# Rotary products of a row issued one head earlier, in an attention and expert kernel on one Trainium2 core

## What is computed

```python
ct_q  = _lin(x, w_down_q, b_down_q)                        # x is the normalised row
q_ct  = _lin(ct_q, w_up_q, b_up_q)
rope_q = _rope(_lin(ct_q, wq_r, bq_r), cos, sin)
q = (q_ct + rope_q).reshape(bs, sl, nh, hd)                # 16 heads of 16
ct_kv = _lin(x, w_down_kv, b_down_kv)
k_ct  = _lin(ct_kv, w_up_k, b_up_k)
rope_k = _rope(_lin(ct_kv, wk_r, bk_r), cos, sin)
k = (k_ct + rope_k).reshape(bs, sl, nh, hd)
v = _lin(ct_kv, w_up_v, b_up_v).reshape(bs, sl, nh, hd)
scores = jnp.einsum('bqhd,bkhd->bhqk', q, k) / np.sqrt(hd)
probs = jax.nn.softmax(scores, axis=-1)
a = jnp.einsum('bhqk,bkhd->bqhd', probs, v)
```

## Time and profile before

| | us |
|---|---|
| median of 3 runs | 497.55 (495.1, 497.55, 499.42) |
| profiled execution, its own time | 496.64 |
| its span in the profile | 494.8 |
| mean granted TensorE clock | 0.97 |
| PE busy | 436.1 (88% of the span) |
| DVE busy | 252.4 (51%) |
| ACT busy | 185.6 (38%) |
| POOL busy | 134.7 (27%) |

### The profile page before, as it was taken

How to read it: one execution, slowest core, us unless ns; L and a number is a source line. 1 busy time by engine, 2 the same in 40 slices (tenths; PEclk the granted TensorE clock), 3 DMA queues, 4 the chain that set the end, 5 groups by cost and what they waited for, 6 DMA issues and landing times.

```text
span 494.8 us, 7794 instructions
## 1 busy us (share of the span) xinstructions
PE 436.1 (88%) x2519; PEld 280.7 (57%) x2520; DVE 252.4 (51%) x591; ACT 185.6 (38%) x383; POOL 134.7 (27%) x195
## 2 busy tenths in 40 slices
PE   3755789999999998989899999999999999999791
PEld 2533456666666664646466565666666666655551
DVE  4243667868686867774867522222222222234665
ACT  1315566666666665545522222222222222221010
POOL 1114141525252515132120011111211110048433
PEclk9977999999999998989999999999999999999897
DMA  8491335363626363601384301111111111123311
GB/s 252 138 93 39 98 77 188 82 198 83 199 73 202 81 190 96 193 1 45 111 275 156 128 23 32 44 42 42 42 45 50 51 44 42 42 86 108 106 42 64
DMA packets 53989, 48.33 MB, mean 98 GB/s; under 512 B 5862, under 2 KB 49638, under 8 KB 53958
## 3 DMA queue, kind: packets, MB, share of 16 engines
q1 hardware_dynamic: 47424, 39.23, 27.3%
q0 software_dynamic: 1872, 5.11, 3.7%
q10 hardware_dynamic: 4662, 3.59, 2.5%
HBM read 25.78 MB, written 9.31 MB: 71 GB/s over the span
## 4 chain that ended last, share of the span: by engine, by line
PE 64%; DVE 15%; POOL 6%; issue 5%; SPq 4%; DMA 3%; ACT 2%; POOLq 0%; ACTq 0%; DVEq 0%
PE bank L1208 42%; PE bank L1212 7%; DVE nmax L946 4%; PE bank L1328 4%; SPq L434 4%; PE bank L1344 3%; PE bank L1292 3%; POOL pv L637 2%; PE bank L1260 2%; PE bank L1268 2%; DMA stacks<-parts_q 2%; DVE wall L976 1%; DVE stats_at L879 1%; POOL rstd_at L535 1%; DVE wall L966 1%
## 5 line engine op out<-in xcount | busy, mean ns | idle before, releaser
L1208 PE MATMUL bank<-wall,stacks 128*128 (+2 forms) x616 | 212.5, 488 | 6.1 <-DVE stacks L1141 5.5
L1208 PEld LDWEIGHTS bank<-wall,stacks 128*128 128x128 f32 x616 | 112.0, 192 | 68.5 <-issue 58.0
L946 DVE TENSOR_REDUCE nmax<-bank 128x2 f32<-128x512 f32 x128 | 85.0, 685 | 52.4 <-PE bank L1292 52.4
L1137 DVE TENSOR_TENSOR stacks<-stacks,bank 128x512 f32<-128x512 f32 x39 | 26.8, 687 | 85.9 <-PE bank L1208 85.9
L1292 PE MATMUL bank<-stacks 96*128 96x256 bf16 x256 | 49.0, 279 | 14.8 <-DMA stacks<-parts_q 8.0
L621 POOL DMA_INDIRECT stacks<-x_sc,row_i x23 | 22.0, 955 | 124.2 <-PE bank L1212 124.2
L821 ACT ACTIVATE stacks<-bank 128x512 f32<-128x512 f32 x39 | 23.3, 597 | 82.5 <-PE bank L1208 82.5
L1344 PE MATMUL bank<-stacks 99*128 99x256 bf16 x256 | 50.3, 280 | 4.4 <-DMA stacks<-mT 2.8
L783 ACT ACTIVATE pv<-bank 128x512 f32<-128x512 f32 x64 | 38.0, 598 | 36.6 <-PE bank L1344 35.7
L1141 DVE COPY stacks<-bank 128x512 f32<-128x512 f32 x39 | 26.9, 690 | 46.4 <-PE bank L1212 46.1
L783 ACT ACTIVATE wall<-bank 128x512 f32<-128x512 f32 x64 | 38.0, 603 | 31.7 <-PE bank L1344 30.8
(11 more groups left out here) (150 smaller groups left out, 513.5 us busy)
## 6 DMA issues: line engine op xcount, KB each, us to landing
wall<-gate_up SPq DMA_DIRECT2D x8, 1024.0 KB, 5.2
stacks<-parts_k SPq DMA_DIRECT2D x96, 64.0 KB, 2.6
stacks<-parts_q SPq DMA_DIRECT2D x91, 64.0 KB, 2.6
wall<-down SPq DMA_DIRECT2D x8, 512.0 KB, 6.2
y_exp<-stacks ACTq DMA_DIRECT2D x23, 128.0 KB, 1.7
x_tok<-wall SPq DMA_DIRECT2D x8, 256.0 KB, 2.6
stacks<-x_tok SPq DMA_DIRECT2D x16, 128.0 KB, 2.3
out<-stacks SPq DMA_DIRECT2D x8, 256.0 KB, 2.2
```

Source lines behind the costliest of these rows:

```text
L946: dve.tensor_reduce(nmax[:, half, qt, 2 * pair:2 * pair + 2], two(sm_bank[u % 2]), AX.X, ALU.max, negate=True).then_inc(sm["sm_max"], 1)
L1137: dve.tensor_tensor(hid, sg, fu[:, :], ALU.mult).then_inc(sm["h_sb"], 1)
L1208: last = pe.matmul(out_ap, lhsT, rhs, start=(n == 0), stop=(n == len(pairs) - 1))
```

## The change

TensorE's table has the rotary products (`A_R`, row b+2 at head 0 of slot b) no more. They stand at head 15 of the slot before, under a name that begins with B (row b+3 at head 15 of slot b), which is the same row. The first query products (`A_Q`) move from head 1 to head 0. `A_R` stays as a name for the prologue and for `MOVED`.

```diff
-            steps = {"B_xnT": a_xnT, "B_ct": a_ct, "B_ct1": lambda b, par: ct_half(b, 1), "A_R": a_rope, "A_Q": a_q,
+            steps = {"B_xnT": a_xnT, "B_ct": a_ct, "B_ct1": lambda b, par: ct_half(b, 1), "A_R": a_rope, "B_R": a_rope,
+                     "A_Q": a_q,
...
-            order = {0: ("A_R",), 1: ("A_Q",), 2: ("M1", "E_xn2T",), 3: ("A_QK",), 4: ("E_router",),
+            order = {0: ("A_Q",), 2: ("M1", "E_xn2T",), 3: ("A_QK",), 4: ("E_router",),
                      6: ("D_avT0",), 8: ("D_avT1", "N_v",), 9: ("D_aT", "B_xnT",), 10: ("D_wo",),
-                     12: ("M0", "B_ct",), 13: ("B_ct1",)}
+                     12: ("M0", "B_ct",), 13: ("B_ct1",), 15: ("B_R",)}
```

## The result

| | before | changed |
|---|---|---|
| median (lowest to highest) | 497.94 (492.56 to 499.86), 8 runs | 502.53 (500.47 to 504.25), 8 runs |
| ratio | | 1.0106, 95% interval 1.0075 to 1.0137 |
| profiled execution, own time (span) | 496.64 (494.8) | 500.81 (499.0) |
| mean granted clock | 0.97 | 0.963 |

A second measurement with 12 runs of the changed kernel beside 23 of the one before gave a ratio of 1.0079 (1.0051 to 1.0108). The change costs 0.8 to 1.1%: it is slower, since both intervals lie above 1, by about the 1% that the prediction took as its line. Forecast were 501.7 us and +4.6 us; the medians of the first measurement differ by 4.6 us, those of the second (501.43 and 498.31) by 3.1 us.

What follows compares the result with a forecast made beforehand. TensorE (PE, busy 88%) was taken as the bound. Per boundary 0.99 + 0.10 + 0.06 = 1.15 us, times 4 = +4.6 us: 501.2 on own time, 502.2 on the median, middle 501.7 us; range 498.2 to 505.5.

Steps and rivals of the forecast that it cites:

- The bound: TensorE's row sets the time; a step moved inside it costs only by waits opened or closed; removal at head 0 gains 0.
- The new wait: At head 15 the rotary products wait for ScalarE's two copies: 0.99 us per boundary, with a hand-over of 0.14 us.
- Starting again: A float32 step on TensorE that starts after a wait takes longer: 0.10 us per boundary.
- Queue behind the waiting step: On PE, later matmuls cannot pass the waiting rotary products; if they could, 1.00 us of value products would cover the wait.
- Crowding: Heads 0, 1 and 2 come closer, so ScalarE's copy of the maxima comes later: 0.06 us per boundary.
- Number of boundaries: The cost falls at slots 1/2, 2/3, 3/4 and 4/5, none at 0/1: 4 x 1.15 = +4.6 us.
- The lower bound: If PE's 0.60 us wait at head 2 were taken back, a boundary costs 0.55 us, +2.2 us in all.
- The DMA at head 0: Rival: head 0's 0.41 us gap is a DMA wait that moved work fills, -2.1 us; chance 0.05.
- Mostly taken back: Rival: earlier ScalarE copies or missed slack recover most of the wait, +0 to +2.2 us; chance 0.17.
- The clock: Rival: new waits drop PE's clock at one to four boundaries, 1.55 us per fall, +6.2 to +10.8 us; chance 0.10.

Runs made afterwards that it cites:

- at head 14: Changed kernel with the rotary products one head earlier still, at head 14 instead of 15, copies unchanged: ratio 1.0137 to the kernel before, slot 26.46 us.

## Why the prediction was right

*The bound.* It said that a step within TensorE's row pays or costs only by the waits that it opens or closes. Putting the rotary products ahead of the products with the values, or behind them, is the difference between 26.02 and 25.12 us.

*The new wait* was worked out as 0.99 us and is 0.89. ScalarE and PE came as foreseen; the hand-over was too long. I took 0.14 us from the transposes at head 2; here it is 172.00 - 171.95 = 0.05 us. This is the term that was mis-sized, 0.4 us of the 4.6.

*Starting again.* 0.10 us was taken and 0.12 is there: from the rotary products to the products with the values are 1.07 us, of which 0.86 are the step and 0.09 the change to these small products (they follow a score unit by 0.32 us, another step follows it by 0.23); 0.12 is left. The reason that I gave is too narrow. With the rotary products behind those with the values their four records took 1.13 us as well, with no wait before them, against 1.03 before. What both cases share is that the weights were not loaded ahead: the load began with the product (172.00 and 172.00; 171.20 and 171.21 behind the products with the values), and in the kernel before 0.11 us ahead of it (172.04 and 172.15). I have not separated that.

*Queue behind the waiting step.* Nothing went round it: the products with the values began after it in the changed kernel and then took their 1.00 us, and at head 14 the scores of head 15 began after it.

*Crowding* was put at 0.06 us; the query products alone gave 0.04 and the difference between both moves and one 0.03.

*Number of boundaries.* Four with the wait and one without, as said. The sum is 4 x 1.03 = 4.12 us instead of 4.6, and 4.12 us are 0.83% of the time before (497.94), inside both intervals.

*The lower bound*, that the 0.60 us at head 2 could be taken back, did not come about: the wait is 0.64 us now.

*The rivals.* The DMA at head 0 holds nothing: the gap of 0.41 us stayed with the transfer long done. Mostly taken back: no, not within the slots. The clock did not fall at the four new waits in any profile: it stayed at 2.4 GHz from slot 1 to slot 5. Behind slot 5 it was at the lower level for 13.7 us in two of three profiles of the changed kernel and 6.8 us in both of before, which makes a difference of 2.3 us in that stage. Against a part of the change in this, the mean granted clock over the timed executions is 0.967 before (65 of them) and 0.968 changed (20), and their medians are 497.56 and 501.72 us, 4.2 us apart. That is the sum of the slots, and with equal mean clocks the stretches at the lower level, at the start too, make no difference on balance. Whether the longer stretch belongs to the change is open: these two have 10.2 us in one piece there, and none of the other ten profiles, the third of the changed kernel among them, has over 3.4 us.

*The chances.* 0.37 stood on slower by over 1% and 0.60 on within 1%. With +0.83% in the slots and ratios of 1.0106 and 1.0079 it lies on that line, where it was put.

## What to carry to other kernels

Before a step is issued earlier on the bounding engine, add up when its operands are ready on the other engine's own row, with what stands ahead of them there (here an exponential and a DMA issue of 0.75 us), and compare with when the bounding engine gets there. If the operands are later, the wait costs its length in every round, less what it takes off a later wait (0.44 us at head 14, nothing at head 15), unless work whose operands are ready stands ahead of the step; here one place later in the row brought the cost from 1.03 to 0.13 us. The same reading finds the gain: the 0.60 us wait that the timeline showed at head 2 was worth 0.45 us in each slot once independent work was put into it.

## What the runs showed of the hardware

- One stage of a kernel can repeat to 0.01 us over several executions (99.23 twice, 103.35 three times) while the whole differs by 8 us (492 to 500). The scatter is in the start, 77.9 to 80.9 us in twelve profiles, in slots 5 to 7 with their stretches of low clock (44.0 to 47.8 us) and in what follows. For a small change that acts in one stage, that stage measured in the trace tells more than a dozen timed runs.
- The hand-over from ScalarE to a waiting matmul differs by place: 0.05 us for the rotary products, 0.14 us for the transposes at head 2.
- A DMA issue of 0.75 us on ScalarE held its row: the next instruction, exponential or copy, began 0.10 to 0.11 us after it, and the trace put the 0.89 us of idle time down to PE, whose products had ended 0.4 us or more before.
- All twelve profiles have the same two waits of 0.84 and 1.08 us (to 0.01) at slots 5/6 and again at slots 6/7. PE's clock went from 2.4 to 1.2 GHz during the second of them or within 6 us behind it in 11 of the 12 at the first place and in 7 at the second, so the waits alone don't decide it. It never did behind the single wait of 1.78 us at head 14, nor behind 0.28 and 0.89 us together.
